# Two transformer layers with modulated norms: norms and gating passed by quarters inside the written-out expert loop

## The chip, the cores and the metric

The kernel runs on one core of a Trainium2 chip. The metric is the device time of one execution in microseconds, the median of the runs. Five engines matter: TensorE (matmuls and transposes, written PE in the profile, its weight loads PEld), VectorE (DVE), ScalarE (ACT), GpSimd (POOL) and SyncE (SP), which only issues transfers. They run side by side, each through its own list of instructions in order, and are tied together by semaphores.

## The reference, cut to what matters

The input is x of 16 x 256 tokens of 128 features. Two layers follow each other; both have the form below, with scale, shift and gate vectors worked out from a condition.

```python
h = _layernorm(x, axis=-1) * (1 + ca) + sa
x = x + ga * _L0_attn_ref(h, ...)          # relative-position attention, 16 heads
h = _layernorm(x, axis=-1) * (1 + cb) + sb
x = x + gb * _L0_ffn_ref(h, ...)           # 8 experts, best two of each token
...
h = _layernorm(x, axis=-1) * (1 + ca) + sa
x = x + ga * _L1_attn_ref(h, ...)          # linear attention, features elu(.) + 1
h = _layernorm(x, axis=-1) * (1 + cb) + sb
x = x + gb * _L1_ffn_ref(h, ...)           # FP4-rounded gated feed-forward

# _L0_ffn_ref
logits = xf @ router_w.T
top_w, top_i = lax.top_k(softmax(logits), 2);  top_w = top_w / sum(top_w)
g = einsum('nd,ehd->neh', xf, w_gate);  u = einsum('nd,ehd->neh', xf, w_up)
y = einsum('neh,edh->ned', silu(g) * u, w_down)
out = einsum('ned,ne->nd', y, combine)     # combine holds top_w, else 0
```

All eight experts are computed for all tokens, and the results are weighed.

## The kernel before, in words

The 4096 tokens lie as 32 tiles of 128 tokens in R2 (NT = 32); four tiles make a chunk of 512 tokens, so there are 8 chunks, and 8 tiles are a quarter. A norm runs over all engines: VectorE's bn_stats and some small steps (statistics, line 1187 on) give mean and variance, GpSimd turns them into an inverse root with a pow (inverse_root, line 480, per half; quarter_root, line 472, per quarter in the first norms), ScalarE centres each tile (L672), VectorE multiplies by the scale (scaled, L1208), GpSimd adds the shift (shifted, L489). TensorE then transposes the chunk (transposes, L879), and ScalarE copies it out of PSUM. Fp16 products are made exact enough by splitting each operand into a high and a low half; each product is then three matmuls (L1026 to L1028).

The change touches this stretch, in order:

1. Front. Behind attention, ScalarE lays out the numerators in OB (L751), TensorE projects a chunk (L1008), VectorE multiplies by the gate into TMP (gate_projection, L1369), GpSimd adds TMP to R2 (residual, L505). When all chunks are through, the norm runs in two halves over HN1; each chunk is transposed and split into XH, high by ScalarE (L756; L757 copies it whole to R1) and low by VectorE (L1385). Then come 64 logit matmuls (L1020, L1021), and the gating on VectorE: some 21 small steps on [128, 32 tiles, 8 experts] (L1389 to L1411), with one exponential of the gap between the two best on ScalarE (L759).

2. The expert loop: tc over 8 chunks, k over 16 halves of hidden units; k = 2e and 2e+1 belong to expert e. On TensorE, experts_up(tc, k) makes gate and up, twelve matmuls for two k; behind each even k, expert_down runs for the pair two before. ScalarE: Silu into SG (L769), then high_hidden of the k before, a copy of HB into the high half of HH (L763). VectorE: hidden_product into HB (L1434), low_hidden into the low half of HH (L1438, HB less the high half), and once per pair weigh, four small instructions that add the expert's output into ACC (L1425, L1426). HB and SG have two buffers, HH four; the waits hb_done, sg_done, h_done, y_mm and acc_done hold them. GpSimd, once per chunk: add_experts (L568, times the gate), combine_weights (L573), expert_residual (L579, into R2). The loop is a hardware loop: Fori(0, 8) on ScalarE, Fori(1, 8) behind a first chunk on TensorE and VectorE, Fori(0, 7) on GpSimd. The order of VectorE in a chunk:

```python
for e in range(E):
    for k in (2 * e, 2 * e + 1):
        hidden_product(tc, k)
        if k:
            low_hidden(tc, k - 1)
    ...
    elif e > 1:
        weigh(tc, e - 2, first)
low_hidden(tc, 15)
```

3. Tail. All wait for moe_added to reach 8. SP then loads the eight tensors of layer 1's attention. The next norm runs in two halves over HN2, the chunks are transposed and copied to R1 (L777), and eight query chunks follow: TensorE (L1071), the exponential on ScalarE (L783), two instructions on VectorE (L1473, L1469). GpSimd adds the projection's bias to R2 beside it (residual_bias, L497). Then keys and values begin (L1479).

## Time and profile before

| | |
|---|---|
| median of 3 runs | 1160.16 us (1160.02 to 1160.19) |
| profiled execution | 1159.43 us, span 1157.6 us |
| TensorE clock granted, mean | 0.868 of full speed |
| TensorE busy | 887.7 us (77%) |
| VectorE busy | 767.8 us (66%) |
| ScalarE busy | 469.9 us (41%) |
| GpSimd busy | 352.9 us (30%) |
| chain that ended last | PE 48%, DVE 22%, ACT 7%, POOL 6% |

The page also cuts the span into 40 slices of some 29 us, each digit the busy share in tenths:

```profile
PE   2474779999999999863799999999738960367774
DVE  6583535556456555247789888888868768976674
ACT  4850223333333333346455555565463124122221
POOL 5551003343343333338101111110182046423332
PEclk7696889999999999876799999999957985588776
```

The line PE is read from the left: preparation, sixteen heads of attention, then a dip around slice 18 and 19 (the front), eight slices of experts, the dip of the tail, and layer 1. VectorE is fullest where the experts run. A busy share is an average over stages; what bounds a stage is seen in its own timeline, and the two dips in PE are stretches in which one engine hands on to the next.

### The profile page before, as it was taken

The numbers are of one execution on the slowest core, as the hardware profiler recorded it, in microseconds if no ns is written. First come the engines' busy times: TensorE is split into PE (matmuls) and PEld (weight loads), VectorE is DVE, ScalarE is ACT, GpSimd is POOL, SyncE is SP. The second block draws the span as 40 slices with busy tenths as digits, with TensorE's granted clock in tenths as the row PEclk, the third lists the DMA queues.
The fourth block names the chain that finished last, engine by engine and source line by source line (L and its number), as shares of the span: only waits on it lengthen the run. The fifth ranks groups of instructions, "written<-read, shape, count | busy, mean of one in ns | idle before, by whom it ended". The sixth has DMA issues, their size and how long they took to land.

```text
span 1157.6 us, 22651 instructions
## 1 busy us (share of the span) xinstructions
PE 887.7 (77%) x8587; PEld 672.9 (58%) x8587; DVE 767.8 (66%) x1570; ACT 469.9 (41%) x764; POOL 352.9 (30%) x388
## 2 busy tenths in 40 slices
PE   2474779999999999863799999999738960367774
PEld 1243668988888888642365655556524860245553
DVE  6583535556456555247789888888868768976674
ACT  4850223333333333346455555565463124122221
POOL 5551003343343333338101111110182046423332
PEclk7696889999999999876799999999957985588776
DMA  5074113332333333520000000000000000000000
GB/s 130 0 211 149 36 34 59 90 72 65 75 82 69 60 94 66 136 49 0 1 1 1 0 0 0 0 0 0 1 16 0 1 14 7 0 5 14 18 18 19
DMA packets 69588, 46.10 MB, mean 40 GB/s; under 512 B 35056, under 2 KB 60856, under 8 KB 68792
## 3 DMA queue, kind: packets, MB, share of 16 engines
q1 hardware_dynamic: 52776, 24.75, 9.4%
q0 software_dynamic: 8032, 19.11, 6.4%
q10 hardware_dynamic: 8704, 1.19, 0.6%
q8 instruction: 52, 0.85, 0.3%
q14 instruction: 24, 0.20, 0.1%
HBM read 30.05 MB, written 12.06 MB: 36 GB/s over the span
## 4 chain that ended last, share of the span: by engine, by line
PE 48%; DVE 22%; ACT 7%; POOL 6%; SPq 6%; issue 5%; DMA 5%; ACTq 1%; DVEq 0%; POOLq 0%
PE PS L949 8%; PE PS L1026 5%; PE PS L1028 5%; PE PS L1027 5%; PE PS L969 5%; PE PS L929 4%; PE PS L953 4%; PE PS L930 4%; DVE HB L1434 2%; SPq L322 2%; PE PS L1146 2%; PE PS L1162 2%; DVE STAT L1191 2%; POOL HN L489 2%; DVE HH L1438 2%
## 5 line engine op out<-in xcount | busy, mean ns | idle before, releaser
L1301 DVE TENSOR_REDUCE MX<-PS 128x2 f32<-128x512 f32 x256 | 171.4, 685 | 171.5 <-PE PS L930 170.1
L726 ACT ACTIVATE REG<-PS 128x1024 f32<-128x1024 f32 x128 | 131.6, 1028 | 240.5 <-PE PS L953 237.7
L949 PE MATMUL PS<-XX,TB 96*128 96x64 f16 x2048 | 160.1, 246 | 6.9 <-DMA XX<-NEG 4.3
L929 PE MATMUL PS<-TM,YY 128*128 128x256 f16 x512 | 128.5, 283 | 33.9 <-DMA YY<-REG 16.9
L949 PEld LDWEIGHTS PS<-XX,TB 96*128 96x128 f16 x2048 | 133.6, 120 | 22.4 <-issue 12.8
L930 PE MATMUL PS<-KM,YY 128*128 128x256 f16 x512 | 125.4, 277 | 0.0
L769 ACT ACTIVATE SG<-PS 128x512 f32<-128x512 f32 x128 | 76.3, 597 | 105.4 <-PE PS L1028 105.0
L1026 PE MATMUL PS<-XH,XX 128*128 (+1 forms) x256 | 98.6, 385 | 15.8 <-DVE HB L1434 15.8
L953 PE MATMUL PS<-XX,KC 97*128 97x128 f16 x1024 | 107.8, 229 | 0.0
L1434 DVE SCALAR_TENSOR_TENSOR HB<-PS,SG 128x512 f32<-128x512 f32 x128 | 87.0, 685 | 31.3 <-ACT SG L769 29.7
L1027 PE MATMUL PS<-XH,XX 128*128 (+1 forms) x256 | 98.3, 384 | 0.0
L1028 PE MATMUL PS<-XH,XX 128*128 (+1 forms) x256 | 98.1, 383 | 0.0
L929 PEld LDWEIGHTS PS<-TM,YY 128*128 128x128 f16 x512 | 73.6, 144 | 40.9 <-issue 17.0
L1438 DVE TENSOR_TENSOR HH<-HB,HH 128x512 f16<-128x512 f32 x128 | 95.2, 744 | 1.5 <-ACT HH L763 1.5
L1026 PE MATMUL PS<-XX,HH 128*128 128x128 f16 x512 | 89.1, 219 | 2.1 <-DVE HH L1438 2.1
L1027 PE MATMUL PS<-XX,HH 128*128 128x128 f16 x512 | 89.1, 219 | 0.0
L1028 PE MATMUL PS<-XX,HH 128*128 128x128 f16 x512 | 89.1, 219 | 0.0
L568 POOL TENSOR_TENSOR ACC<-ACC,MOD 128x512 f32<-128x512 f32 x8 | 10.2, 1270 | 245.6 <-DVE ACC L1426 245.6
L763 ACT ACTIVATE HH<-HB 128x512 f16<-128x512 f32 x128 | 79.8, 623 | 4.9 <-DVE HB L1434 4.9
L953 PEld LDWEIGHTS PS<-XX,KC 97*128 97x128 f16 x1024 | 76.5, 113 | 0.0
L930 PEld LDWEIGHTS PS<-KM,YY 128*128 128x128 f16 x512 | 75.1, 147 | 0.5
L969 PE MATMUL PS<-REG,V 128*32 128x256 f32 x1024 | 62.9, 387 | 1.1 <-ACT REG L726 1.1
(220 smaller groups left out, 1725.7 us busy)
## 6 DMA issues: line engine op xcount, KB each, us to landing
REG<-inverse_sums POOLq DMA_DIRECT2D x60, 128.0 KB, 3.0
YY<-queries_content ACTq DMA_DIRECT2D x224, 4.0 KB
KC<-keys_strips SPq DMA_DIRECT2D x16, 192.0 KB
keys_strips<-REG POOLq DMA_DIRECT2D x12, 224.0 KB, 7.8
R<-in_L_attn_x SPq DMA_DIRECT2D x32, 64.0 KB, 3.2
out<-R SPq DMA_DIRECT2D x64, 32.0 KB, 1.6
queries_position<-REG POOLq DMA_DIRECT2D x2, 960.0 KB, 13.2
queries_content<-REG POOLq DMA_DIRECT2D x2, 960.0 KB, 18.1
```

The lines of the kernel that those rows point to most:

```text
L726: A(P[jt][:, 1024 * up:1024 * up + 1024].rearrange("p (k x) -> p k x", k=2), ST[u % 2], ACT.Exp).then_inc(exp_done, 1)
L929: mm(o, yp[:, a], TM[p][:, 31 - a:31 - a + T], start=True, stop=False)
L930: last = mm(o, yc[:, a], KM[p][:, :], start=False, stop=True)
L949: mm(o_pos[:, a], TB[p][0:96, y0:y0 + 128], xp[0:96, 8 * bank + a], start=(a == 0), stop=False, skip_group_check=True)
L953: last = mm(o[:, 128 * c:128 * c + 128].rearrange("p (b s a) -> p b s a", b=4, s=4), KC[p][0:97, c, 128 * jt:128 * jt + 128], xc[0:97, ban ...
L969: last = mm(PV[32 * g:32 * g + 32, c, :].rearrange("p (q x) -> p q x", q=8), V[:, v0:v0 + 32], p[:, b], start=(jt == 0 and c % 2 == 0), st ...
L1026: mm(o, w[0], x[0], start=first, stop=False)
L1027: mm(o, w[0], x[1], start=False, stop=False)
L1028: return mm(o, w[1], x[0], start=False, stop=final)
L1301: nc.vector.tensor_reduce(MX[h % 2][:, 2 * kk:2 * kk + 2], banks[4 + kk % 2].rearrange("p (a j) -> p a j", a=2), AX_X, ALU.max)\
L1434: STT(HB[k % 2][:, :], banks[2 + k % 2], 1.0 / WS, SG[k % 2][:, :], ALU.mult, ALU.mult).then_inc(hb_done, 1)
L1438: TT(HH[k % 4][:, 1, :], HB[k % 2][:, :], HH[k % 4][:, 0, :], ALU.subtract).then_inc(h_done, 1)
```

## The change

- Front, by quarters. OB and TMP move to another part of REG, since HN1 is now written while the gates still run. GpSimd takes the root of a quarter between the adds; VectorE interleaves gates, quarter_statistics and quarter_modulated, which now holds scale and shift both (the shift was GpSimd's). Only chunks 0 to 3 are transposed and split before the loop. The low half is read from PSUM directly, the copy to R1 falls away.
- Gating by halves: logits(0) before the loop and gating(0) inside chunk 0; logits(1) in chunk 1 and gating(1) in chunks 2 and 3. The exponential becomes a pow with base e on GpSimd (gap_exponential). The last two quarters of norm 3 run inside chunk 0, transposes up to chunk 1.
- The loop is written out on all engines (no Fori). Each engine has a function beside(tc, k) that inserts steps. GpSimd takes the low halves of odd k, and h_done splits into h_even and h_odd.
- The norm behind the experts runs inside the loop for three of its quarters: statistics in chunks 2, 4 and 6 from k = 10, the root at their end, centring (k 1 to 4), scale and shift (k 6 to 9), transposes (k 12, 14) and copies (k 13, 15) in chunks 3, 5 and 7. The last quarter runs between the query chunks.
- Layer 1's weights have their place in YY and are loaded before the last head's sums. Chained steps use Later, which waits before the next step that needs it instead of right behind the step.

```diff
@@ SP @@
                          a["L0_ffn_w_down"].rearrange("e d k -> d e k")).then_inc(ld_moe, 16)
             sp.dma_start(RN[:, :], a["L0_ffn_router_w"]).then_inc(ld_moe, 16)
+            for i, w in enumerate(("wq", "wk", "wv", "wo")):
+                sp.dma_start(L1W[:, i, :], a["L1_attn_" + w]).then_inc(ld_l1, 16)
+            sp.dma_start(BQ1, a["L1_attn_bq"].rearrange("(p o) -> p o", o=1)).then_inc(ld_l1, 16)
+            sp.dma_start(BKV[:, 0:128], a["L1_attn_bk"].partition_broadcast(128)).then_inc(ld_l1, 16)
+            sp.dma_start(BKV[:, 128:256], a["L1_attn_bv"].partition_broadcast(128)).then_inc(ld_l1, 16)
+            sp.dma_start(BO1, a["L1_attn_bo"].partition_broadcast(128)).then_inc(ld_l1, 16)
...
-            sp.wait_ge(moe_added, 8)
-            for i, w in enumerate(("wq", "wk", "wv", "wo")):
...
@@ GpSimd @@
-            residual(o_mul, R2, TMP, o_add)
-            inverse_root(3)
-            shifted(1, HN1, MOD[0][:, 3, :], h_ready)
-
+            for q in range(4):
+                for c in (2 * q, 2 * q + 1):
+                    gp.wait_ge(o_mul, c + 1)
+                    gp.tensor_tensor(R2[:, 4 * c:4 * c + 4, :], TMP[c % 2].rearrange("p (n d) -> p n d", n=4),
+                                     R2[:, 4 * c:4 * c + 4, :], ALU.add).then_inc(o_add, 1)
+                if q:
+                    quarter_root(3, q - 1)
             for e in range(E):
                 gp.memset(RANK[:, :, e], float(E - e)).then_inc(pool, 1)
+            quarter_root(3, 3)
...
+            def gap_exponential(half):
+
+                gap = M1[2][:, 16 * half:16 * half + 16, 0]
+                gp.wait_ge(gap_ready, half + 1)
+                gp.tensor_tensor(gap, LN[:, 6, 16 * half:16 * half + 16], gap, ALU.pow).then_inc(cmb, 1)
+
+            def low_hidden(tc, k):
+
+                gp.wait_ge(hi_done, 16 * tc + k + 1)
+                gp.tensor_tensor(HH[k % 4][:, 1, :], HB[k % 2][:, :], HH[k % 4][:, 0, :], ALU.subtract).then_inc(h_odd, 1)
+
+            for tc in range(8):
+                for e in range(E):
+                    low_hidden(tc, 2 * e + 1)
+                    if tc == 0:
+                        if e == 0:
+                            gap_exponential(0)
+                        elif e == 1:
+                            combine_weights(0)
+                    elif e == 1:
+                        add_experts(tc - 1)
+                        combine_weights(tc)
+                    elif e == 2:
+                        expert_residual(tc - 1)
+                    if tc == 2 and e == 6:
+                        gap_exponential(1)
+                if tc in (2, 4, 6):
+                    quarter_root(4, tc // 2 - 1)
             add_experts(7)
             expert_residual(7)
+            gp.wait_ge(moe_added, 8)
             gp.memset(VN[:, :, :, 128:130], 1.0).then_inc(pool, 1)
-            inverse_root(4)
-            shifted(2, HN2, MOD[1][:, 0, :], h_ready)
+            quarter_root(4, 3)
+            gp.wait_ge(centred, 24)
...
@@ ScalarE @@
+            def centre_tiles(n, dst, tiles):
+
+                act.wait_ge(rstd_ready, turn(n, tiles[0] // 8))
+                for t in tiles:
+                    last = A(dst[:, t, :], R2[:, t, :], ACT.Identity, bias=LN[:, 3, t:t + 1], scale=LN[:, 2, t:t + 1])
+                    if t % 4 == 3:
+                        last.then_inc(centred, 1)
...
             def high_hidden(tc, k):
                 act.wait_ge(hb_done, 16 * tc + k + 3)
                 act.wait_ge(y_mm, 8 * tc + k // 2 + 1)
                 A(HH[k % 4][:, 0, :], HB[k % 2][:, :], ACT.Copy).then_inc(hi_done, 1)
 
-            with act.Fori(0, 8) as tc:
+            def beside(tc, k):
+
+                if tc == 0 and 4 <= k < 8:
+                    centre_tiles(3, HN1, range(24 + 2 * (k - 4), 26 + 2 * (k - 4)))
+                elif tc == 0 and k in (11, 12):
+                    expert_input(k - 7)
+                elif tc == 1 and k in (2, 3):
+                    expert_input(k + 4)
+                elif tc in (3, 5, 7):
+                    q = (tc - 3) // 2
+                    if 1 <= k < 5:
+                        centre_tiles(4, HN2, range(8 * q + 2 * (k - 1), 8 * q + 2 * k))
+                    elif k in (13, 15):
+                        linear_input(2 * q + (k - 13) // 2)
+
+            centre_tiles(3, HN1, range(0, 8))
+            centre_tiles(3, HN1, range(8, 16))
+            expert_input(0)
+            expert_input(1)
+            centre_tiles(3, HN1, range(16, 24))
+            expert_input(2)
+            expert_input(3)
+            for tc in range(8):
                 for k in range(16):
                     act.wait_ge(gu_mm, 16 * tc + k + 1)
                     act.wait_ge(hb_done, 16 * tc + k + 1)
                     A(SG[k % 2][:, :], banks[k % 2][:, :], ACT.Silu, scale=1.0 / WS).then_inc(sg_done, 1)
                     if k:
                         high_hidden(tc, k - 1)
+                    beside(tc, k)
                 high_hidden(tc, 15)
 
...
+            query_exponential(0)
+            query_exponential(1)
+            centre_tiles(4, HN2, range(24, 32))
+            query_exponential(2)
+            query_exponential(3)
+            linear_input(6)
+            linear_input(7)
+            for c in range(4, 8):
+                query_exponential(c)
...
@@ TensorE @@
+            def logits(half):
+
+                pe.wait_ge(x_high, 4 * half + 4)
...
+            def beside(tc, k):
+
+                if tc == 0 and k in (10, 11):
+                    expert_transposes(k - 6)
+                elif tc == 1 and k == 1:
+                    expert_transposes(6)
+                    expert_transposes(7)
+                elif tc == 1 and k == 8:
+                    logits(1)
+                elif tc in (3, 5, 7) and k in (12, 14):
+                    linear_transposes(tc - 3 + (k - 12) // 2)
+
             pe.sem_inc(y_mm, 2)
-
-            def experts(tc, first):
+            for c in range(4):
+                expert_transposes(c)
+            pe.wait_ge(w_low, 13)
+            logits(0)
+            for tc in range(8):
                 for k in range(16):
                     experts_up(tc, k)
                     if k % 2 == 0:
                         if k >= 4:
+                            if tc == 0 and k == 4:
+                                pe.wait_ge(lg_read, 1)
                             expert_down(tc, k // 2 - 2)
-                        elif not first:
+                        elif tc:
                             expert_down(tc - 1, E - 2 + k // 2)
-
-            experts(0, True)
-            with pe.Fori(1, 8) as tc:
-                experts(tc, False)
+                    beside(tc, k)
             expert_down(7, E - 2)
             expert_down(7, E - 1)
 
-
-            transposes(2, HN2)
-            pe.wait_ge(t_evac, 24)
             pe.wait_ge(ld_l1, 128)
             for c in range(8):
+                if c == 4:
+                    linear_transposes(6)
+                    linear_transposes(7)
+                pe.wait_ge(t_evac, 16 + c + 1)
...
@@ VectorE @@
+            def quarter_statistics(q, done, count):
+
+                tiles = slice(8 * q, 8 * q + 8)
+                ve.wait_ge(done, count)
+                for n in range(8 * q, 8 * q + 4):
+                    nc.vector.bn_stats(STAT[:, n, :], R2[:, n, :])
+                yield
+                for n in range(8 * q + 4, 8 * q + 8):
+                    last = nc.vector.bn_stats(STAT[:, n, :], R2[:, n, :])
+                norm(last)
...
+            def quarter_modulated(order, q, dst, scale, shift):
+
+                for c in (2 * q, 2 * q + 1):
+                    t = dst[:, 4 * c:4 * c + 4, :]
+                    ve.wait_ge(centred, 8 * order + c + 1)
+                    norm(TT(t, t, scale.unsqueeze(1).to_broadcast([128, 4, D]), ALU.mult))
+                    yield
+                for c in (2 * q, 2 * q + 1):
+                    t = dst[:, 4 * c:4 * c + 4, :]
+                    norm.wait()
+                    TT(t, t, shift.unsqueeze(1).to_broadcast([128, 4, D]), ALU.add).then_inc(h_ready, 1)
+                    yield
 
...
+                TT(gap, gap, top, ALU.subtract).then_inc(gap_ready, 1)
+                yield
+                ve.wait_ge(cmb, half + 1)
+                gate(TS(total, gap, 1.0, None, ALU.add))
+                yield
+                gate.wait()
...
+            for c in range(4):
+                attention_gate(c)
+            for _ in quarter_statistics(0, o_add, 2):
+                pass
+            for c in range(4, 8):
+                attention_gate(c)
+            for _ in quarter_statistics(1, o_add, 4):
+                pass
+            for _ in quarter_statistics(2, o_add, 6):
+                pass
+            for _ in expert_norm(0):
+                pass
+            for _ in quarter_statistics(3, o_add, 8):
+                pass
+            for _ in expert_norm(1):
+                pass
+            for c in range(4):
+                expert_low(c)
+            first_gating, second_gating = gating(0), gating(1)
+            third_norm, fourth_norm = expert_norm(2), expert_norm(3)
+            next_statistics = [quarter_statistics(q, moe_added, 2 * q + 2) for q in range(4)]
+            next_norm = [linear_norm(q) for q in range(4)]
+
+            def beside(tc, k):
+
+                if tc == 0:
+                    if k < 4:
+                        for _ in range(3 if k < 3 else 2):
+                            next(first_gating)
+                    if k in (4, 5):
+                        for _ in range(9 - k):
+                            next(first_gating)
+                    elif 6 <= k < 10:
+                        next(third_norm)
+                    elif k >= 12:
+                        next(fourth_norm)
+                        if k < 14:
+                            expert_low(k - 8)
+                elif tc == 1 and k in (4, 5):
+                    expert_low(k + 2)
+                elif tc == 2:
+                    next(second_gating)
+                if tc == 3 and k < 4:
+                    next(second_gating)
+                if tc in (2, 4, 6) and k >= 10:
+                    next(next_statistics[tc // 2 - 1])
+                elif tc in (3, 5, 7) and 6 <= k < 10:
+                    next(next_norm[(tc - 3) // 2])
...
-                if not (isinstance(tc, int) and tc == 0 and k < 2):
-                    ve.wait_ge(h_done, 16 * tc + k - 1)
+                if tc or k >= 2:
+                    ve.wait_ge(*((h_odd, 8 * tc + k // 2) if k % 2 else (h_even, 8 * tc + k // 2)))
                 STT(HB[k % 2][:, :], banks[2 + k % 2], 1.0 / WS, SG[k % 2][:, :], ALU.mult, ALU.mult).then_inc(hb_done, 1)
...
                 for e in range(E):
                     for k in (2 * e, 2 * e + 1):
                         hidden_product(tc, k)
-                        if k:
+                        if k % 2:
                             low_hidden(tc, k - 1)
-                    if e == 0 and not first:
+                        beside(tc, k)
+                    if e == 0 and tc:
                         weigh(tc - 1, E - 2)
-                    elif e == 1 and not first:
+                    elif e == 1 and tc:
                         weigh(tc - 1, E - 1)
-                    elif e > 1:
-                        weigh(tc, e - 2, first)
-                low_hidden(tc, 15)
-
-            chunk(0, True)
-            with ve.Fori(1, 8) as tc:
-                chunk(tc, False)
+                    elif e == 3 and tc == 0:
+                        weigh(tc, 0, True)
...
+            query_features(0)
+            query_features(1)
+            for _ in next_statistics[3]:
+                pass
+            query_features(2)
+            query_features(3)
+            for _ in next_norm[3]:
+                pass
+            for c in range(4, 8):
+                query_features(c)
+
```

## Rows read from the trace of the kernel before

**Rows 1.** Busy us by stretch (x instructions), then PEclk, DMA share, GB/s.
```profile
559.40:569.20 9.80, 4.25 (x19) 1.48 (x15) 8.58 (x23) 2.60 (x4) 0.21 (x1) 0.67 0.00 0
...
600.00:633.30 33.30, 31.83 (x290) 19.92 (x289) 29.46 (x66) 19.51 (x34) 3.12 (x3) 1.00 0.00 1
...
834.90:865.30 30.40, 7.22 (x37) 5.20 (x34) 19.65 (x58) 16.97 (x40) 23.38 (x18) 0.61 0.06 15
...
865.30:885.50 20.20, 15.19 (x24) 5.92 (x24) 12.33 (x17) 6.67 (x9) 9.17 (x7) 0.66 0.00 0
```

**Rows 2.** Timeline of VectorE, a pair inside chunk 0: start us, us, what.
```profile
582.23 0.69 DVE L1434 SCALAR_TENSOR_TENSOR HB<-PS,SG 128x512 f32<-128x512 f32 x1 [0.41 <-ACT SG L769]
582.83 0.68 DVE L1438 TENSOR_TENSOR HH<-HB,HH 128x512 f16<-128x512 f32 x1
583.43 1.12 DVE L1426 SCALAR_TENSOR_TENSOR ACC<-PS,CMBT,ACC 128x128 f32<-128x128 f32 x4
584.47 0.68 DVE L1434 SCALAR_TENSOR_TENSOR HB<-PS,SG 128x512 f32<-128x512 f32 x1
...
586.16 0.69 DVE L1434 SCALAR_TENSOR_TENSOR HB<-PS,SG 128x512 f32<-128x512 f32 x1 [0.41 <-ACT SG L769]
```

**Rows 3.** Timeline of TensorE, chunk 2: two up products, a weight load.
```profile
641.91 0.38 PE L1026 MATMUL PS<-XH,XX 128*128 x1
...
642.13 0.38 PE L1027 MATMUL PS<-XH,XX 128*128 x1
...
643.09 0.10 PEld L1026 LDWEIGHTS PS<-XH,XX 128*128 128x128 f16 x1 [0.21 <-DVE HB L1434]
```

**Rows 4.** Timeline of ScalarE: a copy, a turn, Silus of odd k.
```profile
583.38 0.62 ACT L763 ACTIVATE HH<-HB 128x512 f16<-128x512 f32 x1
...
599.32 1.28 ACT L769 ACT_TABLE_LOAD   x1
...
606.24 0.60 ACT L769 ACTIVATE SG<-PS 128x512 f32<-128x512 f32 x1 [1.52 <-PE PS L1028]
...
618.78 0.60 ACT L769 ACTIVATE SG<-PS 128x512 f32<-128x512 f32 x1 [1.52 <-PE PS L1028]
...
639.48 0.60 ACT L769 ACTIVATE SG<-PS 128x512 f32<-128x512 f32 x1 [1.52 <-PE PS L1028]
```

**Rows 5.** Timeline of VectorE, a gate of the first projection.
```profile
522.39 0.69 DVE L1369 TENSOR_TENSOR REG<-PS,MOD 128x512 f32<-128x512 f32 x1 [0.33 <-PE PS L1008]
```

**Rows 6.** Timelines of VectorE, ScalarE and TensorE behind the loop.
```profile
838.97 3.19 DVE L1191 BATCH_NORM_STATS2 STAT<-R 128x6 f32<-128x128 f32 x16 [2.71 <-POOL R L579]
...
846.60 12.42 ACT L672 ACTIVATE HN<-R,LN 128x128 f32<-128x128 f32 x32 [14.65 <-POOL LN L482]
...
859.64 3.56 PE L879 MATMUL PS<-CON,HN 128*128 128x128 f32 x16 [4.80 <-ACT R L777]
...
870.50 3.78 PE L1071 MATMUL PS<-R,L1W 128*128 128x512 f32 x4 [3.22 <-DVE QT L1469]
...
877.90 0.75 DVE L1473 TENSOR_SCALAR RL<-PS,BQ 128x512 f32<-128x512 f32 x1 [1.38 <-ACT EX L783]
```

**Rows 7.** Timelines of GpSimd and VectorE, pow and one product of a norm.
```profile
12.61 1.66 POOL L472 TENSOR_TENSOR LN<-LN 128x8 f32<-128x8 f32 x1 [2.55 <-DVE LN L1201]
...
536.49 2.90 POOL L480 TENSOR_TENSOR LN<-LN 128x16 f32<-128x16 f32 x1 [1.01 <-DVE LN L1201]
...
537.19 0.69 DVE L1208 TENSOR_TENSOR HN<-HN,MOD 128x512 f32<-128x512 f32 x1 [0.78 <-ACT HN L672]
```

**Rows 8.** Timelines of GpSimd and VectorE in chunk 2.
```profile
642.51 1.27 POOL L568 TENSOR_TENSOR ACC<-ACC,MOD 128x512 f32<-128x512 f32 x1 [30.11 <-DVE ACC L1426]
...
642.95 1.38 DVE L1438 TENSOR_TENSOR HH<-HB,HH 128x512 f16<-128x512 f32 x1
```

**Rows 9.** Timelines of TensorE and VectorE: third up product; a 128x128 operation.
```profile
569.26 0.61 PE L1026 MATMUL PS<-XH,XX 128*128 128x512 f16 x1 [5.61 <-DVE HB L1434]
...
906.79 0.28 DVE L1497 TENSOR_TENSOR KVM<-PS,CON 128x128 f32<-128x128 f32 x1
```

246 lines of the change are left out of this document (149 added, 97 removed).

## The prediction

> **What bounds the kernel now.** I first read the busy shares of a few stretches [rows 1]. Inside a chunk of the expert loop TensorE is busy 31.8 of 33.3 us at full clock. In the 9.8 us ahead of it, and in the 30.4 us behind it, it is busy 4.3 and 7.2 us and its clock has come down. So there are three places to look at: the front (attention gates to the first experts), the loop, and the tail (last expert to keys and values).
>
> Next the loop itself, pair by pair. A pair (one expert of one chunk) lasts 3.93 us from one odd product to the next [rows 2], whatever VectorE does, since it idles 0.41 us each time. TensorE's up products follow each other at 0.215 us [rows 3]; twelve of them are 2.59 us, and the 24 down products fill the other 1.34 us. TensorE is the bound, but with no air: the weight load at 643.09 waited 0.21 us for HB. In [rows 2] the chain is: odd product (0.60), low half (0.60), weighing (1.04), even product (0.60), and the even product ends 2.9 us after the odd one began, just when TensorE wants the bank. The odd low half, last in the pair, lies in slack. Hence VectorE has room behind an even product (some 1.1 us, once the odd low is gone) and almost none behind an odd one.
>
> Last the joints. The Silu of k=3 comes at 606.24 and 639.48 [rows 4]: 33.24 us for a chunk that has 8 x 3.93 = 31.44 us of work, so 1.80 us are lost per chunk. From 606.24 to 618.78 are 12.54 us for three pairs of 3.93 us: 0.75 us belong to GpSimd's residual work there; the other 1.05 us lie at the turn, where a table load of 1.28 us stands.
>
> **Front.** The third projection gate starts at 522.39 [rows 5]; from there I count along VectorE, with 0.20 us for one bn_stats (16 in 3.19) and about 1.0 us for the small steps [rows 6], so 2.6 us a quarter. The fourth gate ends at 523.1; statistics of quarter 0 to 525.7; gates 4 and 5 to 526.9. Gate 6 needs GpSimd's fourth add, queued behind the root of quarter 0. A pow of 8 columns is 1.66 us against 2.90 for 16 [rows 7], with its product 2.0 us, and an add of 128x512 is 1.27 us [rows 8], so gates 6 and 7 end at 531.0. Statistics 1 and 2: 536.2. Norm 0 is four instructions of 0.69 us [rows 7] and meets two adds, 540.0; statistics 3: 542.6; norm 1: 545.4; lows 0 and 1: 546.7. Chunks 2 and 3 each go once around TensorE (1.1), ScalarE (0.6) and VectorE (0.65), partly over each other: 549.9. Half the logits: 550.9. The first up product thus starts at 550.9 instead of 559.4. ScalarE's centring of 16 tiles (0.388 us each from 32 in 12.42, [rows 6]) lies beside the adds.
>
> **Chunk 0.** The gating no longer stands ahead of the products: TensorE's third up had to wait until 569.26 for it [rows 9]. It is now 20 steps of half the size, about 0.32 us each by the 0.28 us of a 128x128 operation [rows 9], so 6.4 us, in pairs that have no weighing yet. But step 15 waits for the exponential, which is now a pow of 16 columns on GpSimd (2.90 us, [rows 7]; before it was 0.3 us of ScalarE), and behind the pow on GpSimd are queued the odd low half of the second pair and the weights for the first weighing. From the first up to the end of the up of chunk 1, k=3: 20 ups of 1.29 and 8 downs of 1.35 are 36.6; 1.5 for the slow clock at the start (as in [rows 9]); four transposed groups 3.8; waits 10.5 (2.4 for the first products with the Silu table load, 3.3 for the pow and the low half behind it, 3.3 for gating steps, late weights and two weighings at once, 1.5 for norms and lows at k=12 to 15). That ends at 603.3, against 606.05 before ([rows 4], less the 0.19 us to the Silu): 2.8 us ahead. Most of the 8.5 us won in the front is eaten here.
>
> **Rest of the loop.** Written out, it has no turn with a table load: -6 x 1.05 = -6.3 us. The GpSimd stall: -7 x 0.75 = -5.3, of which I give back 1.5, because GpSimd now works in every pair. Added on TensorE: six groups of transposes at 0.89 us (16 transposes in 3.56, [rows 6]) and half the logits, +6.2. Added on VectorE: what stands behind an even product is free (bn_stats 0.80, norms 0.69, gating 0.32, all under 1.1 us). What stands behind an odd one stalls TensorE by its length less some 0.05 us, but in two pairs running only once, since the chain from up to up spans two pairs: low of chunk 1 0.6, gating steps 1.2, statistics 0.75 x 3, norms 0.6 x 3, and 2.4 where step 15 of the second half waits for its pow (2.90 us from the end of the odd low, less the 0.5 to 1 us by which TensorE runs ahead): +8.3. Sum +4.4 us. The centring on ScalarE (0.78 us per k) moves a Silu to 0.35 us before its product needs it, and costs nothing.
>
> The odd low half on GpSimd: no row has it with an f16 operand. It can start 1.9 us after the odd product began (that ScalarE copy is at 583.38, [rows 4]), and the next odd product needs HB back 3.93 us after, so up to 1.95 us cost nothing. The nearest row, the f32 operation of the same shape, is 1.27 us [rows 8]; I take that. A low of 0.6 us as on VectorE would give nothing more; twice 1.27 is the rival below.
>
> The loop ends at 834.9 - 2.8 + 4.4 = 836.5, 1.6 us later than before: it is paid for by the tail.
>
> **Tail.** Before, 50.6 us lie between 834.9 and 885.5 [rows 1]: moe_added, statistics of 32 tiles, roots, 12.42 us of centring, scale and shift, eight groups of transposes, then eight query chunks. Now, from the last down: weights, banks and R1 are ready, so query chunks 0 and 1 go at once, and after the table load VectorE ends them at +6.2 (0.75 and 0.69 us each, [rows 6]); statistics 3 to +8.8; root +10.9; centring of 8 tiles +14.2. ScalarE has the exponentials of chunks 2 and 3 queued behind that centring, so VectorE stands still from 8.8 to 15. Chunks 2 and 3: +18.6; last norm with GpSimd's eight bias adds beside it: +23.8; two transposed groups and copies: +25; four query chunks at TensorE's slow rate (3.78 us for two, [rows 6]): +34. Against 50.6: -16.6. With the clock back at full speed it would be +32.
>
> The loads of layer 1's eight tensors move in SP's queue ahead of the last head's sums. SP has nothing else to issue until that head's context is out, so I take them as hidden; with that cover gone, eight issues would lie ahead of the last head's chain of transfers (an estimate, 0 to 5 us, kept inside the range). Two more memsets and the moved TMP and OB cost nothing: GpSimd waits for VectorE right behind the memsets, and the buffers change only their place. Written-out code must be fetched where a loop body was repeated; attention, ahead of it, is written out too, and its pairs of weight load and matmul run on, so I take nothing for it.
>
> **Sum.** +1.6 - 16.6 = -15.0 us on the profiled execution, 1159.43 (span 1157.6, 1.8 around it), gives 1144.4; the median of 1160.16 lies 0.73 above that execution, so 1145.2.
>
> **A rule of the Trainium skill.** Where GpSimd adds at 642.51 (1.27 us), VectorE's low half begun at 642.95 takes 1.38 us [rows 8]. SBUF — State Buffer, section "Who interferes with whom", says that an instruction of VectorE with two SBUF inputs and a GpSimd one that reads SBUF exclude each other for the whole instruction; by that rule, this row agrees. But under the pow of 2.90 us at 536.49 a product with two SBUF inputs takes its plain 0.69 [rows 7]; so the trace doesn't bear the rule out for a pow. If it held there too, four roots and two exponentials in and behind the loop would each hold VectorE's next such instruction by about 1 us, and the sum would be 1151 instead of 1145; rival 2 holds that case.
>
> **Rivals.**
> 1. *The loop hides what I charge.* If gating and norms fit into jitter, 8.3 and about 5 of the 10.5 us fall away and the tail runs at +32: 1145 - 15 = 1130. For it: VectorE is busy 29.5 of 33.3 us per chunk [rows 1] and loses 64 low halves of 0.60. Against: the missing air behind odd products [rows 2, 3]. Chance 0.22.
> 2. *The filled loop is worse than I charge.* Every wait of SG, HB and HH crosses three engines in order; small ones (0.15 us in each of 64 pairs by locks that fall on VectorE's even low half, as in [rows 8]) give +9.6: 1155. Locks under the six pows, at 1 us each, would alone give +6: 1151; against them stands the 0.69 us in [rows 7]. Chance 0.20, of it 0.04 for the pows alone.
> 3. *GpSimd becomes the bound.* Odd product, ScalarE copy, GpSimd low half, next odd product is a ring of 1.98 us plus the low half. It decides above 1.95 us; at twice 1.27 = 2.54 us a pair lasts 4.52 us, 64 pairs add 38 us: 1183, slower. A f16 operand is the only reason for it. Chance 0.06.
> 4. *Nothing won:* the front's win is lost in chunk 0, the tail is queued up behind ScalarE's order, and small waits add up to 15 us: 1160. Chance 0.05.
>
> My own forecast has 0.47. A difference under 0.2% (2.3 us) is about what a measurement can't tell from no change. Faster by more: 0.47 + 0.22 + 0.19 (nearly all of rival 2) = 0.88; same 0.03; slower 0.09, from rivals 3, 4 and the end of 2. The range takes in rivals 1 and 2: 1129 to 1157.
>
> **What would show it.** First up product at about 551; no table load between 556 and the tail; a GpSimd row of 128x512 f16 near 1.27 us, 64 times; VectorE waiting about 3 us for GpSimd once in chunk 0 and once late in chunk 2; a plain pair still 3.93 us; last down at 836 to 837; keys and values 34 us behind it. It is wrong if that GpSimd row is over 1.95 us, or if pairs without extra work are longer than 3.93 us.

## The result and the profile after

The changed kernel takes 1142.83 us (median of 4 runs, 1141.32 to 1144.26) against 1160.09 us before; the ratio is 0.9851, with a 95% interval of 0.9839 to 0.9864. The forecast was 1145.2, range 1129 to 1157, faster with 0.88: it held. The profiled execution took 1143.78 us, span 1142.0, against 1159.43 before.

Cut at the joints that the prediction named:

| stretch, us | before | after | change | forecast |
|---|---|---|---|---|
| start of the program to the gate at 522.39 [rows 5] | 522.39 | 523.80 | +1.4 | 0 |
| that gate to the first up product | 37.0 | 28.6 | -8.4 | -8.5 |
| first up to the up of chunk 1, k=3 | 46.65 | 51.2 | +4.6 | +5.75 |
| from there to the last down | 228.85 | 230.8 | +1.95 | +4.4 |
| last down to keys and values | 50.6 | 35.85 | -14.75 | -16.6 |
| what is left, with what lies outside the span | | | -0.4 | 0 |
| sum | | | -15.65 | -15.0 |

Four stretches of the kernel after: the front, the start of chunk 0, 33.3 us inside the loop, and the tail. The columns are those of [rows 1]:

```profile
523.80:551.40 27.60, 8.13 (x48) 6.94 (x48) 22.80 (x77) 15.79 (x33) 16.26 (x22) 0.67 0.00 0
551.40:569.90 18.50, 14.81 (x112) 7.42 (x113) 10.00 (x25) 8.77 (x17) 5.17 (x3) 0.85 0.00 1
600.00:633.30 33.30, 32.98 (x325) 21.09 (x323) 24.48 (x60) 18.40 (x35) 11.86 (x11) 1.00 0.01 2
835.00:870.40 35.40, 15.69 (x32) 6.84 (x30) 22.02 (x39) 10.82 (x19) 17.50 (x14) 0.68 0.00 0
```

(TensorE's busy time is the first figure behind the length.) In the chunk TensorE is now busy 32.98 of 33.3 us, VectorE 24.5 instead of 29.5, and GpSimd has gone from 3.1 to 11.9. The front and the tail have not become dense, they have become shorter.

GpSimd's part of the loop, grouped by line (busy, mean ns of one, then its idle time):

```profile
L608 POOL TENSOR_TENSOR HH<-HB,HH 128x512 f16<-128x512 f32 x64 | 75.6, 1181 | 171.2 <-ACT HH L813 171.2
L585 POOL TENSOR_TENSOR ACC<-ACC,MOD 128x512 f32<-128x512 f32 x7 | 9.0, 1292 | 0.0
L603 POOL TENSOR_TENSOR M<-LN,M 128x16 f32<-128x16 f32 x2 | 5.8, 2906 | 3.9 <-DVE M L1582 3.9
```

The odd low half takes 1.18 us with its f16 operand, not more than the f32 row of [rows 8] (1.27 us). The two pows take 2.9 us as in [rows 7]. Their price shows in VectorE's waits over the loop:

```profile
DVE HB L1682 <- ACT SG L841: 50.7, 47, 4.4
DVE M L1585 <- POOL M L603: 6.3, 2, 3.3
```

VectorE stood twice for a pow, 3.3 us at the longest. The timeline of the first one, GpSimd and then VectorE:

```profile
565.02 2.90 POOL L603 TENSOR_TENSOR M<-LN,M 128x16 f32<-128x16 f32 x1 [3.93 <-DVE M L1582]
567.88 1.15 POOL L608 TENSOR_TENSOR HH<-HB,HH 128x512 f16<-128x512 f32 x1
...
567.96 1.11 DVE L1585 TENSOR_SCALAR M<-M 128x16 f32<-128x16 f32 x1 [3.01 <-POOL M L603]
```

and TensorE behind it:

```profile
569.14 0.22 PE L1125 MATMUL PS<-XX,HH 128*128 128x128 f16 x1 [2.87 <-issue]
```

The low half at 567.88 was queued behind the pow, and the down product at 569.14 needs that low half: it starts when it ends. The step of VectorE behind the pow took 1.11 us instead of 0.18, beside that same low half.

There is a second stall of the same size 7.5 us later. In chunk 0 VectorE does the first two weighings together, behind k=7 (the kernel before does the first of them two k earlier), and the down product that needs the bank of the first one waits:

```profile
576.62 0.22 PE L1125 MATMUL PS<-XX,HH 128*128 128x128 f16 x1 [2.80 <-DVE ACC L1673]
```

The tail, VectorE and then ScalarE and GpSimd:

```profile
849.88 0.75 DVE L1717 TENSOR_SCALAR RL<-PS,YY 128x512 f32<-128x512 f32 x1 [5.84 <-ACT EX L853]
...
853.29 3.41 DVE L1361 TENSOR_TENSOR HN<-HN,MOD 128x512 f32<-128x512 f32 x2
856.74 3.31 DVE L1366 TENSOR_TENSOR HN<-HN,MOD 128x512 f32<-128x512 f32 x2
...
846.09 3.18 ACT L796 ACTIVATE HN<-R,LN 128x128 f32<-128x128 f32 x8 [7.04 <-POOL LN L487]
849.18 1.24 ACT L853 ACTIVATE EX<-PS,YY 128x512 f32<-128x512 f32 x2
...
849.89 12.52 POOL L510 TENSOR_TENSOR R<-R,YY 128x512 f32<-128x512 f32 x8
```

VectorE stands 5.84 us (forecast: 8.8 to 15 us after the last down) for exponentials that ScalarE issues behind its centring, and the four operations of the last norm take 6.7 us beside GpSimd's bias adds, against 0.69 us each in [rows 7].

### The profile page after: what moved, and what is told of

It is laid out like the page before. It is cut to its first block, busy times and chain, and to the rows that moved or that the text cites. A ratio compares the mean times of both kernels' runs of the same rounds, so it can differ in the third digit from the quotient of the medians.

```text
span 1142.0 us, 22164 instructions
## 1 busy us (share of the span) xinstructions
PE 884.3 (77%) x8587; PEld 671.1 (59%) x8587; DVE 734.3 (64%) x1571; ACT 453.7 (40%) x748; POOL 411.9 (36%) x447
## 4 chain that ended last, share of the span: by engine, by line
PE 46%; DVE 23%; DMA 7%; POOL 7%; SPq 6%; ACT 5%; issue 5%; ACTq 0%; POOLq 0%; DVEq 0%
PE PS L1029 7%; PE PS L1125 5%; PE PS L1126 5%; PE PS L1127 5%; PE PS L1049 4%; PE PS L1009 3%; PE PS L1033 3%; PE PS L1010 3%; PE PS L1261 2%; SPq L336 2%; PE PS L1277 2%; DMA REG<-inverse_sums 2%; DVE HB L1682 2%; DVE REG L1479 2%; ACT REG L687 1%
## 5 line engine op out<-in xcount | busy, mean ns | idle before, releaser
L608 POOL TENSOR_TENSOR HH<-HB,HH 128x512 f16<-128x512 f32 x64 | 75.6, 1181 | 171.2 <-ACT HH L813 171.2
L1125 PE MATMUL PS<-XH,XX 128*128 128x512 f16 x256 | 98.8, 386 | 9.1 <-DVE HB L1682 8.9
L1126 PE MATMUL PS<-XH,XX 128*128 128x512 f16 x256 | 98.5, 385 | 0.0
L1127 PE MATMUL PS<-XH,XX 128*128 128x512 f16 x256 | 98.3, 384 | 0.0
L1674 DVE SCALAR_TENSOR_TENSOR ACC<-PS,CMBT,ACC 128x128 f32<-128x128 f32 x224 | 62.6, 342 | 1.5 <-PE PS L1127 1.3
```

What stands on the lines that cost most here:

```text
L1125: mm(o, w[0], x[0], start=first, stop=False)
L1126: mm(o, w[0], x[1], start=False, stop=False)
L1127: return mm(o, w[1], x[0], start=False, stop=final)
```

## How the experiments are read

Eleven kernels were run, each beside the kernel before, each ratio with its 95% interval. Medians of one kernel move by 1 to 3 us between runs, and the traces show where: the gate of [rows 5] comes anywhere from 521.86 to 524.39 us, since attention ahead of it varies. From that gate on the front agrees: the first Silu comes 31.33 to 31.37 us behind it in all eight kernels that share the new front. Chunks of the loop whose code is the same agree to 0.02 us from chunk 1 on.

Two places differ where the code is the same, and with them the granted clock of TensorE. The first is chunk 0. In the kernel after, the clock is low (1.2 GHz, half of full) from ahead of the loop until 4.6 us behind the first up product; in e4 it is low only until 2.7 us behind it, and chunk 0 is 1.65 us shorter. The second lies behind the last Silu. The clock falls after 3.8 to 4.3 us in after, e1, e3 and e4, and VectorE's first query step comes 9.4 to 9.9 us behind that Silu; in e2, e7 and e11 it falls after 9.6 to 9.8 us, and the step comes 8.0 us behind. There is one trace of each kernel, so a difference of 2 us or less that includes one of these two places is not settled by it.

Beside the ratio stands the time from that gate to the first of keys and values, with its three parts.

| kernel | median us | ratio to before | gate to keys/values | gate to first Silu | first to last Silu | last Silu to keys/values |
|---|---|---|---|---|---|---|
| before | 1160.1 | 1 | 363.1 | 45.0 | 262.6 | 55.5 |
| e5 written out | 1155.8 | 0.9968 [0.9956, 0.9979] | 359.6 | 45.1 | 259.0 | 55.6 |
| e6 and odd lows on GpSimd | 1147.7 | 0.9899 [0.9879, 0.9918] | 349.7 | 45.2 | 249.9 | 54.6 |
| e9 after, expert inputs ahead | 1144.9 | 0.9866 [0.9850, 0.9883] | 348.6 | 46.0 | 261.9 | 40.8 |
| after | 1142.8 | 0.9851 [0.9839, 0.9864] | 346.4 | 31.3 | 274.1 | 41.1 |
| e1 after, odd lows on VectorE | 1146.0 | 0.9875 [0.9857, 0.9892] | 350.4 | 31.3 | 277.7 | 41.4 |
| e8 after, GpSimd low twice | 1163.0 | 1.0028 [1.0015, 1.0041] | 367.0 | 31.4 | 295.0 | 40.6 |
| e2 after, exponential covered | 1136.6 | 0.9798 [0.9782, 0.9814] | 339.5 | 31.4 | 268.4 | 39.7 |
| e3 after, tail order | 1136.9 | 0.9799 [0.9783, 0.9816] | 340.1 | 31.3 | 273.9 | 34.8 |
| e4 after, bias adds later | 1141.5 | 0.9840 [0.9819, 0.9862] | 342.5 | 31.4 | 272.4 | 38.7 |
| e7 = e2 + e3 + e4 | 1131.0 | 0.9750 [0.9718, 0.9781] | 332.9 | 31.4 | 268.4 | 33.2 |
| e11 = e2 + e3 | 1130.5 | 0.9742 [0.9723, 0.9761] | 332.8 | 31.4 | 268.1 | 33.3 |
| e10 = e9 + e3 | 1139.0 | 0.9824 [0.9787, 0.9860] | 341.3 | 46.0 | 262.0 | 33.3 |

## What the loop gained: written out, and with the odd low half moved

The first edit to the kernel before, and the one on top of it:

```diff
-            with ve.Fori(1, 8) as tc:
+            for tc in range(1, 8):
```

(the same on TensorE, ScalarE and GpSimd)

```diff
+            def low_hidden(tc, k):
+                gp.wait_ge(hi_done, 16 * tc + k + 1)
+                gp.tensor_tensor(HH[k % 4][:, 1, :], HB[k % 2][:, :], HH[k % 4][:, 0, :], ALU.subtract).then_inc(h_odd, 1)
...
-                        if k:
+                        if k % 2:
                             low_hidden(tc, k - 1)
...
-                low_hidden(tc, 15)
```

> The kernel before with nothing changed but its loops over the chunks, which are written out on TensorE, VectorE, ScalarE and GpSimd. The prediction's theory: a turn of the loop costs 1.05 us, because a table load of 1.28 us stands at each; written out these loads are gone, so six to seven turns give 6.3 to 7.4 us back: 1153 to 1154 us, with a period of about 32.2 us from a chunk's Silu to the next one's instead of 33.24. Rival (the turn is hidden, and the win of the change is made elsewhere): within 1 us of the kernel before.

> The kernel before with its loops written out and the low halves of odd k on GpSimd, in the order of the changed kernel; norms and gating stay where they were. Theory: the plain pair stays 3.93 us, since TensorE bounds it, but VectorE's room of 0.60 us takes up what GpSimd's residual work cost (0.75 us per chunk, 5.3 us, of which I gave 1.5 back to contention): a further 4 us below the kernel that is only written out, so about 1149 us, and a chunk of 31.7 us. Rival A (the odd low was in slack and its move carries nothing): within 1 us of the kernel that is only written out. Rival B (GpSimd working in every pair disturbs VectorE's even lows by 0.15 us each): 5 to 9 us slower than that kernel.

Measured: written out 3.5 us less by the traces, a chunk of 32.74 us instead of 33.24; half of what was expected. With the odd lows on GpSimd a further 9.9 us (8 by the ratios; 9.1 inside the loop), twice what was expected, and a chunk of 31.44 us. Pair by pair (Silu of an odd k to the next): the kernel before has one pair of 4.98 and one of 4.68 us in each chunk behind the first, all others 3.93; written out they are 4.42 and 4.74; with the odd lows on GpSimd all are 3.93. TensorE's up products over the loop, before, e5 and e6, by line (the last figure is its idle time for HB):

```profile
L1026 PE MATMUL PS<-XH,XX 128*128 (+1 forms) x252 | 96.4, 382 | 15.8 <-DVE HB L1434 15.8
```
```profile
L1026 PE MATMUL PS<-XH,XX 128*128 128x512 f16 x252 | 96.4, 383 | 12.3 <-DVE HB L1434 12.3
```
```profile
L1037 PE MATMUL PS<-XH,XX 128*128 128x512 f16 x251 | 95.9, 382 | 5.8 <-DVE HB L1446 5.8
```

A chunk of e6 has no idle time left on TensorE (31.44 busy of 31.44):

```profile
600.00:631.44 31.44, 31.44 (x289) 20.10 (x288) 23.37 (x57) 17.85 (x32) 11.88 (x12) 1.00 0.01 1
```

So the 1.05 us of a turn, which the prediction put down to the table load, was two things: 0.56 us (a pair of 4.98 became 4.42) went with the written-out loop, whose trace has one table load where that of before has eight, and 0.50 us was VectorE. In the kernel before, ScalarE and then VectorE at a turn:

```profile
632.57 1.28 ACT L769 ACT_TABLE_LOAD   x1
633.87 1.23 ACT L769 ACTIVATE SG<-PS 128x512 f32<-128x512 f32 x2
...
634.59 1.29 DVE L1434 SCALAR_TENSOR_TENSOR HB<-PS,SG 128x512 f32<-128x512 f32 x2 [0.47 <-ACT SG L769]
```

The first Silu starts when the load ends, VectorE's product waits for it, and TensorE then stands 0.88 us for HB, against 0.32 us written out. The load is thus on the path. No run has the loop without the load, so a cost of the loop's own branch is not ruled out. The timeline of e5 at a turn:

```profile
631.30 1.12 DVE L1426 SCALAR_TENSOR_TENSOR ACC<-PS,CMBT,ACC 128x128 f32<-128x128 f32 x4
632.34 0.68 DVE L1438 TENSOR_TENSOR HH<-HB,HH 128x512 f16<-128x512 f32 x1
632.94 0.68 DVE L1434 SCALAR_TENSOR_TENSOR HB<-PS,SG 128x512 f32<-128x512 f32 x1
```

The low half of k=15 stands ahead of the next chunk's first product, where every other odd low half stands behind it: the even product comes 2.84 us behind the odd one at 630.10, not 2.24, and TensorE waits. The other stall, 0.80 us in the pair with GpSimd's adds, is the lows' meeting with them; in e5:

```profile
640.92 1.26 POOL L568 TENSOR_TENSOR ACC<-ACC,MOD 128x512 f32<-128x512 f32 x1 [29.62 <-DVE ACC L1426]
...
641.29 1.44 DVE L1438 TENSOR_TENSOR HH<-HB,HH 128x512 f16<-128x512 f32 x1
```

In e6 each add follows an odd low half on GpSimd's own queue (638.72, then 639.84), and there VectorE has only an instruction with one SBUF input to run: its even low lasts 0.68 us. The move does not merely shorten VectorE's list, it also spaces GpSimd's adds away from the lows.

## What the odd low half is worth in the changed kernel, and where it would bind

```diff
-                    low_hidden(tc, 2 * e + 1)
...
-                        if k % 2:
-                            low_hidden(tc, k - 1)
+                        if k or tc:
+                            low_hidden(tc - (k == 0), (k - 1) % 16)
```

(The first line is GpSimd's, the others are VectorE's. The low half of k=15 now stands behind the next chunk's first product too, where the kernel before has it ahead. GpSimd then also waits for its own earlier residual add ahead of the next product for ACC, which it has done by then.)

> The changed kernel with the low halves of odd k back on VectorE, where the kernel before has them (behind the next product); all else as changed. Theory: norms, statistics and gating steps no longer find room behind an even product, and each of the eight turns of a chunk loses some of its air: 3 to 9 us slower than the changed kernel, but less waiting behind the two exponentials of GpSimd, since no low half is queued behind them. Rival (GpSimd's part carries nothing, VectorE had the room anyway): within 1 us of the changed kernel.

Measured: 4.0 us slower from gate to keys and values; the ratios (0.9875 against 0.9851) say 2.8, with intervals that just overlap. That is the lower end of what was expected. Chunks 1, 3, 4 to 7 are each 0.85 to 1.08 us longer, but chunk 0 is 1.68 us and chunk 2 0.22 us shorter: those hold the pows, which now delay no low half.

The expected cause, air lost in each of the eight turns of a chunk, was not there. In chunk 4, 0.80 of the 1.08 us are the pair with GpSimd's adds (4.73 for 3.93 us), 0.28 the pair with the statistics (4.87 for 4.59), and the other pairs stay at 3.93. The pair of the turn is one of them: with the low half of k=15 behind the product, the 0.50 us of e5 is gone though VectorE does all the lows. Beside the add of 1.27 us, the odd low half is the one that meets it:

```profile
707.89 1.45 DVE L1687 TENSOR_TENSOR HH<-HB,HH 128x512 f16<-128x512 f32 x1
```

So of the two stalls that e6 took away, that of the turn also goes with another order on VectorE alone; that at the adds is back as soon as the odd low half is. The 9.9 us of e6 and these 4.0 us are nearly the same edit with different neighbours.

```diff
                 gp.wait_ge(hi_done, 16 * tc + k + 1)
+                gp.tensor_tensor(SCR[:, :], HB[k % 2][:, :], HH[k % 4][:, 0, :], ALU.subtract)
                 gp.tensor_tensor(HH[k % 4][:, 1, :], HB[k % 2][:, :], HH[k % 4][:, 0, :], ALU.subtract).then_inc(h_odd, 1)
```

> The changed kernel with one more subtraction of the same size and operands on GpSimd ahead of each odd low half, into a buffer that nothing reads. The two together take about 2.3 us where the prediction put the free limit at 1.95 us. Theory (the ring from odd product over ScalarE's copy and GpSimd to the next odd product decides above that limit): the pair grows from 3.93 to about 4.3 us, 64 pairs add 20 to 25 us, less where pairs were longer already: 15 to 25 us slower than the changed kernel. Rival A (GpSimd's low half has more slack than the ring says): at most 2 us slower. Rival B (there was no slack, each nanosecond counts): 64 x 1.16 = 74 us slower.

Measured: 20.5 us slower. Where the ring decides, it reads so (GpSimd's two, then VectorE's odd products):

```profile
715.68 1.16 POOL L609 TENSOR_TENSOR SCR<-HB,HH 128x512 f16<-128x512 f32 x1 [1.95 <-ACT HH L815]
716.80 1.16 POOL L610 TENSOR_TENSOR HH<-HB,HH 128x512 f16<-128x512 f32 x1
...
713.85 0.69 DVE L1684 SCALAR_TENSOR_TENSOR HB<-PS,SG 128x512 f32<-128x512 f32 x1 [0.97 <-ACT SG L843]
...
718.07 0.69 DVE L1684 SCALAR_TENSOR_TENSOR HB<-PS,SG 128x512 f32<-128x512 f32 x1 [1.30 <-POOL HH L610]
```

From the odd product at 713.85 are 1.83 us to GpSimd's first, 2.28 for the two, 0.11 to the next odd product: 4.22 us, a fixed part of 1.94 and so 1.99 us free (prediction: 1.98 and 1.95). But that happens once. In the next pair the odd product is late and the Silu ahead of ScalarE's copy is not: that Silu starts 0.35 us behind the product (718.42) instead of 0.64, and the copy right behind it comes sooner:

```profile
719.62 1.16 POOL L609 TENSOR_TENSOR SCR<-HB,HH 128x512 f16<-128x512 f32 x1 [1.65 <-ACT HH L815]
...
722.00 0.69 DVE L1684 SCALAR_TENSOR_TENSOR HB<-PS,SG 128x512 f32<-128x512 f32 x1 [1.00 <-POOL HH L610]
```

GpSimd starts 1.55 us behind the product at 718.07, and the pair is back at 3.93. So a steady ring is free up to 3.93 - 1.55 - 0.11 = 2.27 us, and the doubled low half just about fits. The 20.5 us lie where GpSimd has something beside it. The stretch from k=3 of chunk 4 to k=3 of chunk 5, which holds statistics and a root but no gating, grew from 32.10 to 34.50 us: pairs of 4.14 and 4.55 us at the adds, 4.13 and 4.70 (4.59 before) at the statistics, 5.19 behind the root, and the other three at 3.93; chunks 0, 2 and 3, with the pows and the gating, grew by 3.7 to 4.0 us each. The size came out as expected, but the ring alone isn't its cause.

## The two stalls that the prediction had named

```diff
                     if tc == 0:
-                        if e == 0:
+                        if e == 1:
                             gap_exponential(0)
...
-                    if k in (4, 5):
-                        for _ in range(9 - k):
+                    if k in (4, 6, 7):
+                        for _ in range(3):
                             next(first_gating)
...
-                elif tc == 2:
+                elif tc == 2 and k < 14:
                     next(second_gating)
```

(with what follows it in chunk 0 set 2 k later)

> The changed kernel with the gating's steps behind the exponential set two to three k later, so that GpSimd's pow of 16 columns (2.90 us) lies beside a whole pair of products before VectorE needs it, in both halves; the steps are the same. Theory: in the changed kernel VectorE stands 3.01 and 3.30 us before the step behind the pow and TensorE runs dry there (pairs of 9.16 and 5.18 us); with the pow covered 3 to 5.5 us of it come back: about 1138 to 1140 us, and VectorE's wait for GpSimd at that line is gone. Rival (the stall moves: the later steps push weights and inputs of chunk 1, and something else is late by as much): within 1 us of the changed kernel.

Measured: 6.9 us less from gate to keys and values. Chunk 0 up to k=3 of chunk 1 is 3.3 us shorter, chunk 2 1.7, chunk 3 0.5: together 5.6 us, the upper end of what was expected. The other 1.3 us are in the tail, where this edit changes nothing; there the clock stayed full 5.5 us longer behind the last Silu, as told above. VectorE's wait for the pow has left the list of waits.

The stall of the first weighing is still there. The pair of 9.16 us is still 9.10, and in e11, the fastest kernel:

```profile
573.82 0.22 PE L1125 MATMUL PS<-XX,HH 128*128 128x128 f16 x1 [3.35 <-DVE ACC L1673]
```

There the first weighing waits for the weights, whose steps now stand later. But in e9 (below), with the gating done ahead of the loop, the same product still stands 1.84 us, because the weighings are queued behind k=7; its pair is 5.93 us, and 3.93 in e6, which has the first weighing behind k=5. That order was not changed by itself in any run, so how much of this stall can be won back is not shown.

```diff
             query_exponential(1)
-            centre_tiles(4, HN2, range(24, 32))
             query_exponential(2)
             query_exponential(3)
+            centre_tiles(4, HN2, range(24, 32))
```

> The changed kernel with one pair of ScalarE's steps exchanged in the tail: the exponentials of query chunks 2 and 3 stand ahead of the centring of the last eight tiles instead of behind it. Theory: VectorE stood 5.84 us before 849.88 because those exponentials were queued behind the centring; its work for the two chunks (some 3.5 us) now lies in that gap, and the last norm follows the centring at once: 3.5 to 5 us faster than the changed kernel. Rival (that gap is hidden by the slow TensorE and the norm's own waits): within 1 us.

Measured: 6.4 us less, more than the 3.5 to 5 expected. VectorE's norm in this kernel:

```profile
847.45 0.69 DVE L1361 TENSOR_TENSOR HN<-HN,MOD 128x512 f32<-128x512 f32 x1 [0.95 <-ACT HN L796]
848.98 0.69 DVE L1361 TENSOR_TENSOR HN<-HN,MOD 128x512 f32<-128x512 f32 x1 [0.84 <-ACT HN L796]
849.71 2.50 DVE L1366 TENSOR_TENSOR HN<-HN,MOD 128x512 f32<-128x512 f32 x2
```

It also starts before GpSimd's adds (850.07), so only its second half meets them: one edit takes both stalls. That is why the next one adds nothing to it.

```diff
             quarter_root(4, 3)
-            gp.wait_ge(centred, 24)
+            gp.wait_ge(h_ready, 24)
```

> The changed kernel with GpSimd's eight bias adds of the tail waiting until VectorE's last norm is done, instead of running beside it. Theory: beside them each of the norm's four operations took 3.3 to 3.4 us for two, against 0.69 us for one elsewhere (6.7 us for the four, 2.8 alone), and the norm is on the path to the keys and values: 3 to 4 us faster than the changed kernel. Rival (the bias adds are themselves next on the path, so what the norm wins they lose): within 1 us, or slower by up to 3 us if GpSimd's 12.5 us of adds end later than the keys and values need them.

Measured: 4.0 us less by the traces (1.3 by the ratios, whose intervals leave room for both), of it 2.35 in the tail: the norm takes 2.6 instead of 6.7 us, and the bias adds, which now start 26.9 us behind the last Silu instead of 20.7, meet the last query products instead, which take 1.42, 0.98, 1.79 and 0.98 us for 0.69. The other 1.65 us are in chunk 0, where this edit changes nothing; its full clock began 2.7 us behind the first up product instead of 4.6, the up products up to k=3 of chunk 1 took 1.4 us less, and the two pairs around the pow fell as 8.64 and 6.54 us for 6.96 and 9.16. So only the 2.35 us belong to the edit.

> The changed kernel with the three edits together: the exponentials of the gating covered, ScalarE's exponentials of query chunks 2 and 3 ahead of the centring, GpSimd's bias adds behind the last norm. Theory: the stalls lie behind each other on one path, so the three wins add up: 9 to 13 us faster than the changed kernel, 1130 to 1134 us. Rival (the two tail edits free the same time, since the norm can't start before the centring is done): 6 to 8 us.

> The changed kernel with the gating's exponentials covered and ScalarE's exponentials of query chunks 2 and 3 ahead of the centring; GpSimd's bias adds as in the changed kernel. Theory: the bias adds behind the norm bring nothing once the norm starts 6 us earlier than they do, so this is within 1 us of the kernel with all three edits, and 12 us faster than the changed kernel. Rival (the late bias adds do win 1 to 3 us there): slower than the kernel with all three by so much.

Measured: 13.5 us less with all three, 13.6 with two; e4 adds nothing to e3, as the theory of e11 said. Some 1.3 us of both are the clock behind the last Silu, as in e2. The kernel with two edits is the fastest of all: 1130.5 us, 2.6% below the kernel before and 12 us below the changed kernel.

## What the move of the expert inputs into the loop won

The changed kernel with all of the expert inputs and the gating ahead of the loop again, cut to its core:

```diff
-            for c in range(4):
+            for c in range(8):
                 expert_transposes(c)
...
-                if tc == 0 and k in (10, 11):
-                    expert_transposes(k - 6)
...
+            act.wait_ge(gap_ready, 1)
+            A(M1[2][:, :, :], M1[2][:, :, :], ACT.Exp).then_inc(cmb, 1)
...
-            first_gating, second_gating = gating(0), gating(1)
-            third_norm, fourth_norm = expert_norm(2), expert_norm(3)
```

In place of the last two lines stand the norms, the low halves and the gating of the kernel before, in one piece.

> The changed kernel with the part on the expert inputs taken back: all four norms, eight transposed groups, eight low halves, one set of logits and the gating in one piece with ScalarE's exponential stand ahead of the first product, as in the kernel before; loops written out, odd low halves on GpSimd and the next layer's quarters inside the loop stay. Theory from the runs so far: the kernel before, written out and with the odd low halves on GpSimd, takes 249.9 us from its first Silu to its last, the changed kernel 274.0; the three quarters of the next layer's norms cost 2.9 us each in the loop, so this one should take 249.9 + 8.8 = 258.7 us, 15.3 less than the changed kernel, and its first Silu comes about 12 us later (567.1 against 555.1): 3 us faster than the changed kernel, so the move into the loop won nothing as it stands. Rival (the prediction: front 8.5 us ahead, of which 2.8 are left after chunk 0, and only 2.4 for the pow and about 1 for the gating's other steps later): 0 to 1 us faster or slower. Second rival (the early start does pay): 3 us or more slower than the changed kernel.

Measured: 2.1 us slower than the changed kernel by the traces (0.9866 against 0.9851, intervals that overlap). My theory, 3 us faster, fell. Its loop took 261.9 us where the sum said 258.7, and all of the 3.2 us are in chunk 0: a first pair of 6.94 us (5.67 in e6), which waits for the gating's end and meets a low clock, and one of 5.93 us, in which TensorE stands 1.84 us for the first weighing, queued behind k=7 as in the changed kernel. The rest agrees, but the first Silu comes 14.6 us later, not 12: I had taken the 12 from the start of the program, where the two gates stand 1.9 us apart, and the norms by quarters cost 0.8 us more ahead of the loop than those by halves. So the move of the expert inputs wins 14.6 in front, gives 12.2 back inside the loop, and 0.3 in the tail: 2.1 us. That is no more than chunk 0 and the tail differ between traces of the same code, and the intervals overlap, so whether the move as it stands wins anything is not shown. With the pow covered (e2) the same move wins 9 us (8 by the ratios), which is clear. The chunks of e9 give the price of the next layer's quarters too: 0.67 us for a chunk with statistics and 2.26 for one with norm and transposes, 2.9 us each for three of them, against 14.75 us saved in the tail.

> The kernel with the expert inputs ahead of the loop, and ScalarE's exponentials of query chunks 2 and 3 ahead of the centring. Theory: the tail is the same as in the kernel where only this order was changed, so a further 6 us less; with the 3 us above about 1134 us. Rival: the two interact, since the clock of TensorE at the loop's end differs: more than 2 us beside that.

Measured: 7.2 us less than e9 (e3 against after: 6.4), so the tail's edit is worth about the same whatever stands ahead of the loop (5.9 us by the medians); the 1134 us were built on the 3 us that fell, and it was 1139.0.

## The prediction, point by point

- *Front.* 28.6 us for 28.5. Two steps of 128x8 on VectorE lasted 1.29 and 1.13 us beside GpSimd's adds instead of 0.17, which the prediction didn't have; other steps made up for them.
- *Chunk 0.* 51.2 us for 52.4, with luck in the sum. TensorE's waits were 7.85 us for 10.5: the pow with the low half queued behind it 2.87 for 3.3, gating steps and the first weighings 3.2 for 3.3, the first products 0.7 for 2.4, the last norm and lows 1.1 for 1.5. The four transposed groups took 1.75 us for 3.8. Against that stood the clock: it was low for 4.6 us at the start and again from 577.5 to 580.9, behind the two stalls, and the ups and downs took 41.6 us, 5.0 more than their 36.6, some 4 of it the low clock, where the prediction had 1.5.
- *Rest of the loop.* +1.95 for +4.4 us. What I let the loop win was 10.1 us over this stretch (6.3 + 5.3 - 1.5). Here the step on the turn failed in its cause: 1.05 us was right, the table load was about half of it, and written out alone the kernel got 3.5 us, not 6.3. It came right in the sum since the other half was an odd low half, which this change moves as well. From e6 the stretch wins 11.5 us, so the 1.5 us given back to GpSimd's work in every pair were not there. What I added, 14.5 us (6.2 on TensorE, 8.3 of stalls), measured 13.2 (225.4 us from the Silu of chunk 1, k=3, to the last in the changed kernel, 212.2 in e6). Inside it both terms were off: the added work is 3.5 us (2.7 for six transposed groups, 0.8 for the logits), since the row of [rows 6] behind the 0.89 us a group stood at the low clock and a group takes 0.44 at the full one, and what is left for the stalls is 9.7 us.
- *Odd low half.* 1.18 for 1.27 us; the free limit of 1.95 us was too low (1.99 once, 2.27 in a steady row of pairs).
- *Tail.* 35.85 for 34 us. VectorE's idle time was there. The mis-sized term is the norm beside the bias adds: 6.7 us, where I had 5.2; it ends 25.6 us behind the last down (forecast 23.8), and from there to the keys and values are 10.2 us, as forecast.
- *Loads and written-out code.* The loads ahead of the last head's sums left no mark that could be told from attention's own spread of 2.5 us; the +1.4 us there is inside it. The gate stands at 523.1 us in the mean of the ten kernels with the early loads and at 522.1 in that of the three without, which hints at 1 us, but no run changes the loads alone. No stretch shows a cost of code, though the page counts 65 packets of instructions for 52 (e5 has 65 too).
- *The rule of the Trainium skill.* The four steps of the last norm took 1.7 us each beside GpSimd's adds, where 0.69 is plain, and VectorE's step at 567.96 took 1.11 for 0.18 beside the low half. Under a pow VectorE shows nothing of the kind: in e7, GpSimd, then VectorE,

```profile
563.59 2.90 POOL L603 TENSOR_TENSOR M<-LN,M 128x16 f32<-128x16 f32 x1 [0.44 <-DVE M L1582]
...
564.68 0.68 DVE L1686 TENSOR_TENSOR HH<-HB,HH 128x512 f16<-128x512 f32 x1
```

  The page SBUF — State Buffer of the Trainium skill, section "Who interferes with whom", states that an instruction of VectorE with two SBUF inputs and one of GpSimd that reads SBUF exclude each other, and that tensor_scalar can hold the shared ports too. The rows beside adds and low halves agree, those under a pow don't, as [rows 7] had it; the case of 1151 us within rival 2 is out. It is the pow that can be longer: begun beside a norm's two-input product, the pow of 8 columns lasts 2.03 us (539.73 in the changed kernel) instead of 1.65.
- *Rivals.* The free loop (1130) was wrong: TensorE's added work can't be hidden, and stalls of 9.7 us came with it. Rival 2 had its small waits in the wrong place: e6 has pairs of 3.93 us throughout with GpSimd in each. Rival 3 fell with 1.18 us. Its 38 us were too many as well: by the ring of e8, free up to 2.27 us, a low half of 2.54 us would lengthen a plain pair by 0.27 us and not 0.59 (an estimate). Rival 4's queued tail was real and worth 6.4 us (e3), but already in the forecast.
